# Two heads side by side in the rows of TensorE, with attention rows moved in one hop

## The reference

```python
x = x + 0.5 * ffn(layernorm(x), w_gate, w_up, w_down)      # 256 -> 768 -> 256, silu(gate) * up, weights int / 127
x = x + attn(layernorm(x), Wq, Wk, Wv, Wo, bo)
x = x + 0.5 * ffn(layernorm(x), w_gate, w_up, w_down)
# attn: 16 heads of 16 channels
scores = einsum('bhld,bhsd->bhls', qh, kh) * 16 ** -0.5 - slopes[h] * abs(pos_s - pos_l)
out = softmax(scores, axis=-1) @ vh      # then @ Wo.T + bo
```

## Time and profile before

| what | value |
|---|---|
| median of 3 runs | 903.22 us (902.56 to 903.54) |
| the profiled execution's own time | 903.27 us |
| its span, first to last instruction | 901.5 us |
| mean granted TensorE clock | 0.98 of 2.4 GHz |
| busy: PE / DVE / ACT / POOL | 842.3 / 653.9 / 527.9 / 427.2 us |
| first exp of the first turn | at 208.95 us |
| last exp | at 740.50 us |

### The profile page before, as it was taken

One profiled execution on the slowest core, in us unless ns is written; L12 is line 12 of the kernel. 1 busy time (PEld: TensorE's weight loads), 2 busy tenths in 40 slices (PEclk: granted clock), 3 DMA queues, 4 the chain that ended last, 5 costly groups with the idle time before them and its releaser, 6 DMA issues.

```text
span 901.5 us, 13262 instructions
## 1 busy us (share of the span) xinstructions
PE 842.3 (93%) x4672; PEld 577.1 (64%) x4672; DVE 653.9 (73%) x1359; ACT 527.9 (59%) x745; POOL 427.2 (47%) x486
## 2 busy tenths in 40 slices
PE   3899999869999999999999999999998998999997
PEld 2788888734655665665665565565564446888886
DVE  6799888477677677777677677677778725677874
ACT  4344434415658668758758767767766684444443
POOL 0444434423635645645644644644644465334443
PEclk9999999967999999999999999999999999999999
DMA  9220000274482482482482482383383000010001
GB/s 384 72 76 13 2 3 3 49 213 115 96 224 58 105 221 53 100 225 54 95 223 61 90 228 60 85 225 68 81 227 70 1 2 2 26 49 26 25 26 48
DMA packets 37086, 85.24 MB, mean 95 GB/s; under 512 B 3746, under 2 KB 4770, under 8 KB 36818
## 3 DMA queue, kind: packets, MB, share of 16 engines
q1 hardware_dynamic: 36482, 83.45, 34.8%
q10 hardware_dynamic: 512, 0.53, 0.2%
HBM read 45.68 MB, written 38.87 MB: 94 GB/s over the span
## 4 chain that ended last, share of the span: by engine, by line
PE 76%; DVE 9%; DMA 8%; ACT 2%; issue 2%; SPq 1%; POOL 1%; ACTq 0%; DVEq 0%
PE ps L975 70%; DVE row_max L885 4%; DMA k_aug<-parts_scratch 3%; DMA q_aug<-max_row 3%; DMA parts_scratch<-parts 2%; DVE hid L781 1%; PE ps L987 1%; PE ps L1031 1%; PE ps L1026 1%; ACT gated L588 1%; PE ps L1012 1%; PE ps L1036 1%; DVE max_in L896 1%; DVE w_max L838 1%; SPq L425 0%
## 5 line engine op out<-in xcount | busy, mean ns | idle before, releaser
L885 DVE TENSOR_REDUCE row_max<-ps 128x1 f32<-128x512 f32 x512 | 341.3, 687 | 123.6 <-PE ps L975 122.0
L676 ACT ACTIVATE probs<-ps 128x1024 f32<-128x1024 f32 x256 | 252.5, 1022 | 96.5 <-PE ps L975 95.0
L553 POOL TENSOR_TENSOR probs<-probs,diag 128x256 f32<-128x256 f32 x256 | 187.7, 736 | 230.9 <-ACT probs L676 230.6
L975 PE MATMUL ps<-k_aug,q_aug 96*128 96x512 f32 x512 | 222.6, 459 | 12.4 <-DVE row_max L885 6.2
L486 POOL TENSOR_TENSOR hid_r<-hid,hid_r 128x512 fp32r<-128x512 f32 x96 | 124.6, 1299 | 172.8 <-ACT hid_r L582 171.4
L975 PE MATMUL ps<-xnt,wgu_r 128*128 128x512 f32 x768 | 187.5, 399 | 14.6 <-DVE hid L781 10.4
L975 PEld LDWEIGHTS ps<-k_aug,q_aug 96*128 96x128 f32 x512 | 95.6, 194 | 145.7 <-DVE row_max L885 118.7
L975 PEld LDWEIGHTS ps<-xnt,wgu_r 128*128 128x128 f32 x768 | 144.4, 192 | 52.3 <-DVE hid L781 17.6
L975 PE MATMUL ps<-q_aug,k_aug 98*128 98x512 f32 x512 | 159.3, 404 | 6.1 <-DMA q_aug<-max_row 6.0
L975 PE MATMUL ps<-probs,v_aug 128*32 128x512 f32 x1024 | 136.9, 607 | 0.8 <-POOL probs L553 0.8
L588 ACT ACTIVATE gated<-ps 128x512 f32<-128x512 f32 x96 | 57.6, 600 | 114.4 <-PE ps L975 114.4
(11 more groups left out here) (62 smaller groups left out, 690.4 us busy)
## 6 DMA issues: line engine op xcount, KB each, us to landing
parts_scratch<-parts SPq DMA_DIRECT2D x128, 256.0 KB, 5.9
q_aug<-parts_scratch SPq DMA_DIRECT2D x32, 512.0 KB, 4.9
k_aug<-parts_scratch SPq DMA_DIRECT2D x32, 512.0 KB, 6.6
x_sb<-x_in SPq DMA_DIRECT2D x8, 512.0 KB, 12.7
x_out<-x_sb SPq DMA_DIRECT2D x8, 512.0 KB, 2.6
wgu_i<-w_gate_up SPq DMA_DIRECT2D x2, 768.0 KB, 6.2
k_aug<-k_rows_scratch SPq DMA_DIRECT2D x1, 1088.0 KB
w_att<-w_att SPq DMA_DIRECT2D x1, 1024.0 KB, 11.5
```

What stands on the lines that cost most here:

```text
L553: nc.gpsimd.tensor_tensor(tile, tile, diag[:, n * QH + 2 * pair:n * QH + 2 * pair + 2, :], ALU.mult).then_inc(fixed, 1)
L676: nc.scalar.activation(probs[:, kt % 2, 2 * pair:2 * pair + 2, :], ps[:, at:at + 2, :], ACT.Exp).then_inc(exp_done, 1)
L885: nc.vector.reduce_max(row_max[:, quad % 2, u % TT, u // TT:u // TT + 1], max_bank(b, tile)[0], mybir.AxisListType.X).then_inc(s1_used, 1)
L975: return nc.tensor.matmul(out, lhs, rhs, start=start, stop=stop, **k)
```

## The change

- **Two heads in the rows.** q and k keep three of four products, 48 rows. The 6 segments (42 or 43 tokens) have centres such that, with slopes in units of a power of two, no high/low pair is needed: 12 bias rows. With 2 maxima rows a head has 62 rows, 60 without. Head i of a pair sits at partition 64 i, so that the two score matmuls of a step, and two maxima tiles in a row, use different halves of the array's rows. Head order changes (`head_of`), the unit of the slope goes into ACT's exp and a per-partition scale of q (`q_scale`), and the diagonal table has two forms.
- **One hop, two buffers.** `move_rows` copies from `parts` straight into the rows: six DMAs for each qk fill (2 halves of the array x 3 terms, 16 partitions each). `q_aug` and `k_aug` alternate by batch (8 pairs each, total size as before); `parts` has one buffer.
- **Maxima.** The turn of a quad's maxima is one transpose into 32 rows of 128 instead of four into 8 of 512. The two DMAs move from ACT's queue to SP's (`move_max`).
- **Order.** `MAX_LEAD` stays 28. Fills have other steps, the tiles come in twos, `apply_kept` serves b + 2 in steps (1, 2) to (1, 5), batch 1 before the first turn. The first norms of the second feed-forward block move from turn 7 to turn 6 (`first_rows`). POOL places three quads of values in step (3, 7).

The diff, cut:

```diff
-SEG = 64
-NSEG = L // SEG
-ROW_BIAS = 4 * D
-ROW_MAX = ROW_BIAS + 4 * NSEG
+NSEG = 6
+HALVES = (0, 43, 85)
+TERMS = 3
+ROW_BIAS = TERMS * D
+ROW_MAX = ROW_BIAS + 2 * NSEG
 ROWS = ROW_MAX + 2
-PUTS = 16 * 4
+GROUP = 64
+NP = H // 2
+CHUNKS = 2
+MOVES = 16 * 2 * TERMS
...
+def head_of(n, j, i):
+
+    return QH * n + j + 2 * i
+
+
+HEADS_IN_ORDER = [head_of(n, j, i) for n in range(NQ) for j in range(2) for i in range(2)]
+SLOPE_UNITS = [float(slopes()[0]), 1.0]
...
-    (0, 3): "heads3_prev", (0, 5): "max1", (0, 6): "xt0_next", (0, 7): "xt1_next",
-    (1, 1): "turn1_prev", (1, 2): "qk0_next", (1, 3): "qk1_next", (1, 5): "heads0", (1, 6): "max2",
-    (1, 7): "qk2_next",
-    (2, 1): "qk3_next", (2, 2): "v0_next", (2, 3): "heads1", (2, 5): "max3", (2, 6): "v1_next",
-    (2, 7): "out0_prev",
-    (3, 1): "out1_prev", (3, 3): "heads2", (3, 5): "max0_next", (3, 7): "turn0",
+    (0, 0): "xt0_next", (0, 1): "xt1_next", (0, 3): "heads3_prev", (0, 4): "max1", (0, 5): "qk0_next",
+    (0, 6): "qk1_next", (0, 7): "turn1_prev", (1, 1): "out0_prev", (1, 3): "heads0", (1, 5): "max2",
+    (1, 6): "out1_prev", (2, 3): "heads1", (2, 4): "max3", (2, 5): "qk2_next", (2, 6): "qk3_next",
+    (2, 7): "turn0", (3, 1): "v0_next", (3, 3): "heads2", (3, 4): "v1_next", (3, 5): "max0_next",
...
-WEIGHT_SCORES, WEIGHT_VALUES = 2, 4.4
-LN_SHARE = 0.8
-WEIGHTS = {"heads": 2, "max": 2, "turn": 2, "xt": 2, "qk": 6, "v": 6, "out": 6}
+WEIGHT_SCORES, WEIGHT_VALUES = 0.6, 1.0
+WEIGHTS = {"heads": 0.6, "max": 0.2, "turn": 0.55, "xt": 0.55, "qk": 1.4, "v": 1.7, "out": 1.7}
...
-            until = int(MAX_TILES * done / whole + 1e-6)
+            until = 2 * int(MAX_TILES // 2 * done / whole + 1e-6)
...
+        q_aug = [sb(f"q_aug{side}", [P, NP, L], F32R) for side in range(2)]
...
+        k_aug = [k_aug0, sb("k_aug1", [P, NP, L], F32R)]
...
-            def put_parts(quad, of=(0, 1)):
-
-                these = slice((quad % 2) * QH * D, (quad % 2 + 1) * QH * D)
-                for is_k in of:
-                    for twice in range(2):
-                        rows = slice(twice, 4, 2) if is_k else slice(2 * twice, 2 * twice + 2)
-                        sp.dma_start(d_parts[quad, is_k, :, rows, :], parts[quad // 2][these, is_k, :, :].bitcast(F32)
-                                     ).then_inc(parts_out, 16)
-
-            def get_rows(quad, count):
-
-                sp.wait_ge(parts_out, PUTS * count)
-                for is_k, aug in ((0, q_aug), (1, k_aug)):
-                    sp.dma_start(aug[0:ROW_BIAS, quad * QH:(quad + 1) * QH, :].bitcast(F32),
-                                 d_parts[quad, is_k].rearrange("(h d) r t -> (d r) h t", h=QH)
-                                 ).then_inc(aug_done[quad], 16)
-
-            for quad in range(NQ):
...
+            def lay_rows(side):
+
+                for i in range(2):
+                    sp.dma_start(q_aug[side][i * GROUP + ROW_BIAS:i * GROUP + ROW_MAX, :, :].bitcast(F32), d_qrows[i]
+                                 ).then_inc(aug_in[side], 16)
+                    sp.dma_start(k_aug[side][i * GROUP + ROW_BIAS:i * GROUP + ROWS, :, :].bitcast(F32),
+                                 d_krows.rearrange("r (o t) -> r o t", o=1).to_broadcast([ROWS - ROW_BIAS, NP, L])
+                                 ).then_inc(aug_in[side], 16)
+
+            def move_rows(b, name):
+
+                seq, kind, part = fill_parts(b, name)
+                chunk, is_k = part // 2, part % 2
+                wait_done(sp, b, name)
+                pairs = slice(chunk * NP // CHUNKS, (chunk + 1) * NP // CHUNKS)
+                for i in range(2):
+                    for term, half in enumerate((0, 0, 1) if is_k else (0, 1, 0)):
+                        at = i * GROUP + term * D
+                        to = (k_aug if is_k else q_aug)[seq % 2][at:at + D, pairs, :].bitcast(F32)
+                        sp.dma_start(to.rearrange("p q t -> p (q t)"),
+                                     parts[i * GROUP:(i + 1) * GROUP, is_k, half, :].bitcast(F32)
+                                     ).then_inc(rows_moved[is_k], 16)
+
+            def move_max(b, name):
+
+                seq, kind, part = fill_parts(b, name)
+                sp.wait_ge(drained, fill_no(b, name) + 1)
+                for i in range(2):
+                    at = i * GROUP + ROW_MAX
+                    sp.dma_start(q_aug[seq % 2][at:at + 2, 2 * part:2 * part + 2, :].bitcast(F32).rearrange("o j (t p) -> o (j t) p", p=P),
+                                 max_row[i * 4 * TT:(i + 1) * 4 * TT, :].bitcast(F32)
+                                 ).then_inc(max_moved, 16)
+
+            lay_rows(0)
+            for part in range(4):
+                move_rows(-1, f"qk{part}_next")
+            move_max(-1, "max0_next")
+            sp.wait_ge(ffn[0]["y_used"], 2 * B)
+            lay_rows(1)
+
+            for b in range(B):
+                move_max(b, "max1")
+                if not last(b):
+                    wait(sp, st_done, b * (NQ * STEPS))
+                    for part in range(2):
+                        move_rows(b, f"qk{part}_next")
+                move_max(b, "max2")
+                move_max(b, "max3")
+                if not last(b):
+                    for part in range(2, 4):
+                        move_rows(b, f"qk{part}_next")
+                    move_max(b, "max0_next")
...
+                        if (n, s) == (3, 7) and not last(b):
+                            pool.wait_ge(pv_done, b * (NQ * TT) + 3 * TT)
...
-                    nc.scalar.activation(stage[:, slot_of(b, name), :], bank, ACT.Copy,
-                                         scale=D ** -0.5 if kind == "qk" and part % 2 == 0 else 1.0
-                                         ).then_inc(drained, 1)
+                    if kind == "qk" and part % 2 == 0:
+                        nc.scalar.activation(stage[:, slot_of(b, name), :], bank, ACT.Identity, scale=q_scale[:, 0:1]
+                                             ).then_inc(drained, 1)
+                    else:
+                        nc.scalar.copy(stage[:, slot_of(b, name), :], bank).then_inc(drained, 1)
...
-                    nc.scalar.copy(max_row[:, :], bank[0:2 * QH, :]).then_inc(drained, 1)
-
-                    act.wait_ge(drained, at + 1)
-                    for i in range(2):
-                        act.dma_start(q_aug[ROW_MAX + i:ROW_MAX + i + 1, part * QH:(part + 1) * QH, :].bitcast(F32),
-                                      max_row[i * QH:(i + 1) * QH, :].bitcast(F32)).then_inc(max_moved, 16)
-
+                    nc.scalar.copy(max_row[:, :], bank[0:2 * TT * QH, 0:P]).then_inc(drained, 1)
...
-                                             ACT.Exp).then_inc(exp_done, 1)
+                                             ACT.Exp, scale=SLOPE_UNITS[pair]).then_inc(exp_done, 1)
...
-            row_maxima(0, -MAX_LEAD, 0)
...
+            row_maxima(0, -MAX_LEAD, 4 - MAX_LEAD)
+            apply_kept(1, range(TT))
+            row_maxima(0, 4 - MAX_LEAD, 0)
...
+                        if n == 1 and 2 <= s < 6:
+                            if b + 2 < B:
+                                apply_kept(b + 2, (s - 2,))
+                            elif b + 2 == B:
+                                first_rows(s - 2)
+                        row_maxima(b, made, made + count // 2)
+                        row_maxima(b, made + count // 2, made + count)
...
-                    for t in tiles:
-                        ins = nc.tensor.transpose(bank[0:2 * QH, t * P:(t + 1) * P], max_in[:, t, :], eye[:])
+                    if halves[0] == 0:
+                        ins = nc.tensor.transpose(bank[0:2 * TT * QH, 0:P], max_in[:].rearrange("p i o j t -> p (i o j t)"), eye[:])
...
-                    h, t = quad * QH + u // TT, u % TT
-                    if u == 0:
-                        pe.wait_ge(aug_done[quad], (seq + 1) * (16 * 2))
+                    pair, t, rows = 2 * quad + u // STEPS, (u % STEPS) // 2, u % 2 * GROUP
+                    if u == 0 and quad == 0 and seq < 2:
+                        pe.wait_ge(aug_in[seq], 16 * 4)
+                    if u == 0 and quad % 2 == 0:
+                        for moved in rows_moved:
+                            pe.wait_ge(moved, (seq * CHUNKS + quad // 2 + 1) * MOVES)
                     bank, back = max_bank(b, tile)
                     wait(pe, s1_used, b * MAX_TILES + tile + 1 - back)
-                    matmul(bank, q_aug[0:ROW_MAX, h, t * P:(t + 1) * P], k_aug[0:ROW_MAX, h, :],
-                           True, True).then_inc(s1_done, 1)
+                    matmul(bank, q_aug[seq % 2][rows:rows + ROW_MAX, pair, t * P:(t + 1) * P],
+                           k_aug[seq % 2][rows:rows + ROW_MAX, pair, :], True, True).then_inc(s1_done, 1)
...
-            for name in FILLS_BEFORE[2:-1]:
-                fill(-1, name)
-            pe.wait_ge(aug_in, 16 * 2)
-            pe.wait_ge(drained, fill_no(-1, FILLS_BEFORE[-1]))
+            fill(-1, "v0_next")
```

(11 more changed lines are left out.)

196 lines of the change are left out of this document (79 added, 117 removed).

## The result

The changed kernel takes 932.31 us, the median of 4 runs (929.44 to 935.75), against 902.89: a ratio of 1.0328, 95% interval 1.0286 to 1.037. It is 29 us slower where 56 were to be saved. The profiled execution took 935.75 us, its span is 934.0.

The account below looks back on a forecast made before the run. PE was taken to bound the kernel before; after the change, the two-bank cycle of the maxima tiles. Seven turns save 46.2 us, the last turn 8, the lead-in 2: 903.3 - 56 = 847 us, range 808 to 890.

Parts of the forecast that it names:

- A pair costs as much as one matmul, 0.24. I take 0.24: PE's 64 score and maxima pairs per turn: both matmuls run at once, saving 15.4 us a turn.
- The first rival: Pairs on PE do not run side by side, 0.48 us each: 920 us, slower, 12% chance.
- Each costs 0 to 0.10 us; I take 0.10: 38 more changes of PE's array layout per turn, at 0.10 us each: +3.8 us a turn.
- PE's own work is 52.2: PE's work in a turn without waits: 65.1 - 15.4 + 3.8 - 1.3 = 52.2 us.
- The new wait: Maxima tiles in twos hold both banks 1.93 us, 32 times: 61.8 us a turn; 61.5 taken.
- the second rival: DVE is kept fed, reductions nearly without pause, turns of 54 to 57 us: 801 us, 14% chance.
- If the clock fell within turns, all of it would be wrong: Sign to check in the new profile: granted clock still 1.00 within turns.
- Moved `xn` and `first_rows` cost the same where they stand: DVE's `xn` and first norms, moved to other steps, cost the same there as before.
- The last turn, 47.5: The last turn falls from 55.5 to 47.5 us: -8, bounds -3 and -12.
- The lead-in, -2: Before the first turn: rows earlier -3.6, four `xn` +2.2, clock -0.9; taken as -2, bounds 0 and -4.
- Rows in one hop, cost 0: 24 moves and 8 maxima DMAs per turn on SP are hidden: cost 0, bounded at 4 us.
- the third rival: Rows or maxima come late by 4 us more than the cover, turn 65.5 us: 880 us, 12% chance.

Follow-up runs that it names:

- experiment 2: The change with both tiles of each two in the same half of the array's rows, so they cannot overlap: 953.55 us, 1.0565 to the kernel before.
- experiment 3: The kernel before with scores contracted over 62 rows and maxima tiles over 60, adding only layout changes: 990.75 us, 1.0785.
- experiment 13: The change with POOL's four output bias additions spread one each over (2,0), (2,2), (2,4), (2,6) instead of together at (1,0): 915.65 us, 1.0142.
- whole array (4): The change with every score and maxima matmul contracted over all 128 rows, nothing side by side: 928.04 us, 1.0285 to the kernel before.
- Experiment 6: The change with DVE's maximum of each tile taken over 256 of its 512 columns: 879.94 us, 0.9747 to the kernel before.
- whole array, half the reduction (7): The change with scores and tiles over all 128 rows and maxima over 256 of 512 columns: 895.55 us, 0.9901 to the kernel before.
- Experiment 11: The change with the two tiles of a two parted by adjoining scores (tile, score, score, tile): 923.04 us, 1.0184 to the kernel before.
- experiment 10: The change with `first_rows` spread over 22 steps of turn 6 instead of four: 924.6 us, 1.0248 to the kernel before.
- experiment 12: The change with tiles parted by scores, `first_rows` spread over turn 6 and `out0_prev` moved to (1, 2): 901.12 us, 0.9971 to the kernel before.
- Experiment 8: The change with eight moves per qk fill instead of twelve, the third term's rows from a table: 934.76 us, 1.0394 to the kernel before.
- experiment 9: The kernel before with one transpose for a quad's maxima instead of four: 902.73 us, 1.0007.
- 14: The change with tiles parted, `first_rows` spread, `out0_prev` at (1, 2) and POOL's bias additions spread: 891.98 us, 0.9863 to the kernel before.

## Why the prediction was wrong, point by point

**"A pair costs as much as one matmul, 0.24. I take 0.24": right.** The first rival (one after another, 920 us) is out: starts lie 4 ns apart, and experiment 2, without the overlap of the tiles, is 21 us slower. In the trace of the change, a pair between two others is followed by the next 0.235 us later where nothing is waited for, as one matmul of before is. Behind values or whole-array work it takes 0.34, ahead of them 0.33: the price of the layout, the same as for a single matmul in experiment 3 (0.337 and 0.324). The estimate from the Trainium skill ("TensorE: Matmul & The Clock Gate", Part 3), 0.31, does not hold for two halves here.

**"Each costs 0 to 0.10 us; I take 0.10": mis-sized,** 0.18 by experiment 3: 38 x 0.08 = 3.0 us of a turn. My own rows had both sides, 0.33 ahead of values and 0.34 behind them, and I took one of them as the price of a whole change and as its bound. The Trainium skill's rule ("TensorEngine Tiling (Array Packing)", Key Properties) that a change of tiling mode drains the array agrees with this: each of the two changes around a half-row tile costs time on both of its sides.

**"PE's own work is 52.2": it is 56.1.** I price each start by what its kind takes where nothing is waited for (0.234 for 512 columns or a pair of them, 0.118 for 256, 0.109 for a transpose, 1.00 for eight values) and by the two sides of a change. For experiment 3, whose PE hardly waits, this gives 75.9 against 75.8 measured. By kernel, PE's own work in a turn, what is left for waits, and the turn:

| kernel | own work | waits | turn |
|---|---|---|---|
| before | 65.5 | 2.6 | 68.1 |
| the change at full clock (experiment 13) | 56.1 | 12.2 | 68.3 |
| whole array (4) | 64.1 | 6.2 | 70.3 |
| the change, half the reduction (6; some 3.4 us at 1.2 GHz) | 56.1 | 8.8 | 64.9 |
| whole array, half the reduction (7) | 64.1 | 2.8 | 66.95 |

So the array trick does what it should: 8.0 us less work of PE than with the whole array (64.1 against 56.1), layouts included. But 6.0 of these go into waits with the real reductions, and 5.9 with the quick ones.

**"The new wait": the step that failed.** I took the turn as the longer of two cycles over its whole length, 61.5: PE's own work, 52.2, and that of the two banks, 32 x 1.93 = 61.8. But the two bound each gap between two twos by itself, and what one gap has over is not given to the next. With the prices above, PE brings 0.80 to 2.76 us of its own work to a gap of experiment 13, in 11 of 32 gaps more than 1.93; the longer of the two, gap by gap, sums to 64.9, not 61.8. The turn is 68.3. Of the 3.4 still missing, 1.7 is the hole at `out0_prev`, which my walk had missed; the rest is not traced; DVE's work between its reductions (41.8 of its 49.8 us are reductions) is a candidate. In all PE waits 12.2 us of a turn, where 61.5 - 52.2 left it 9.3. Experiment 6 shows that the reductions hold a good part of these waits: with quicker ones 8.8 are left, and the turn is 64.85 instead of 70.7. Experiment 11 gives little of it back by order alone. DVE busy 49.8 of 68.3 us also puts an end to the second rival (801 us).

**"If the clock fell within turns, all of it would be wrong": it fell,** and no chance was given to it. It costs 2.4 of a turn (experiment 13), about 17 us in all. I had read 1.00 in the turns of before and taken it as given, although the change puts more holes and half-row matmuls into PE's time.

**"Moved `xn` and `first_rows` cost the same where they stand": failed for `first_rows`.** In four steps of turn 6 they delay the reductions behind them in DVE's order, and PE with them: 77.8 instead of 69.9 (experiment 10), 8 us.

**"The last turn, 47.5": failed, 54.9.** It gained 0.7 instead of 8; it has the same layouts and bank waits, and a clock of 0.94. In the version of experiment 12 it is 49.2.

**"The lead-in, -2": failed, +4.6.** The last issue leaves SP at 181.8, and the landing takes 8 us, not 3.3:

```profile
174.01 3.88 SPq L442 DMA_DIRECT2D q_aug<-parts  x6
177.93 3.83 SPq L442 DMA_DIRECT2D k_aug<-parts  x6
```

```profile
189.85 1.22 PE L977 MATMUL ps<-k_aug,q_aug 60*128 60x512 f32 x4 [6.81 <-DMA k_aug<-parts]
```

(The moves on SP, and the first tile on PE: 189.85 where I had 183.5.) I took one put's landing for that of twelve moves in a row. Experiment 8, with four moves less, brings the tile 6.0 us forward: its last issue leaves SP at 178.5, 3.3 earlier, and the landing takes 5.4 instead of 8.1. The four `xn` take 2.7, near the 2.2 I gave. The other gain that I counted there, a clock kept up, turned into its opposite: the low stretch lasts until 224.6 us, 213.7 before.

**"Rows in one hop, cost 0": right** within turns. PE's only wait for `k_aug<-parts` is the one of 6.8 us in the lead-in, and the third rival is out.

**"Maxima transposes, -1.3": about right** by experiment 9 (0.7 to 1.0 in turns 3 to 6).

Added up against the forecast: a turn of 68.3 at full clock, 3.9 from PE's own work and 2.9 from more waits, is 7 x 6.8 = 48 us; the clock 17, `first_rows` 8 (some of both fall together), the last turn 7, the lead-in 7, the rest behind it 2. That is 89; the miss was 85 in the median, 88 in the profiled execution.

**What stays open.** Why spreading POOL's additions keeps the clock up. Whether the half-row matmuls themselves bring it down: experiments 3 and 4 (1.2 GHz for long with half-row matmuls, 3.4 us with whole ones) speak for it, but experiments 12 to 14 use half rows too and lose only 6.8, 20.5 and 17.1 us. Separate banks for four tiles in flight, which would test the bank waits directly, were not tried.

## What to carry to other kernels

Matmuls side by side in the rows do run at the price of one (0.235 a pair between equal layouts), but each switch between half-row and whole-array work costs 0.18, on both of its sides: count the switches beside the pairs. When two engines hand few buffers to and fro and both work in order, take the longer of the two gap by gap and add these up; don't compare the two sums. Small work laid in a lump on a side engine was worth 8 us (norms on DVE) and 17 us (bias additions on POOL, by way of the clock and unexplained) when spread one per step; the array trick itself is worth 2.0 us of a turn at full clock, 14 in all.
